# Two scaled fp16 parts for the relation matrices, the product with u as two more fold columns, and 84 instead of 90 table supertiles in a relational GNN layer

## The reference, cut to what matters

```
V = weight.reshape(in_dim, num_bases, out_dim)
W_rel = jnp.matmul(w_comp, V).reshape(num_rels, in_dim, out_dim)
h_src = h[src]
e = jnp.concatenate([h_src @ Ws.T, he @ Ws.T, h[dst] @ Ws.T], axis=1) @ Wa.T
msg = jnp.einsum('ei,eio->eo', h_src, W_rel[rel_type]) * e
h_out = jax.ops.segment_sum(msg, dst, num_segments=n_nodes)
```

## Time and profile before

| | |
|---|---|
| runs | 3934.55, 3935.9, 3939.48 us; median 3935.9 |
| profiled execution | 3944.19 us, its span 3940.3 us |
| mean granted TensorE clock | 0.951 |
| busy share of the span | PE 90%, DVE 72%, POOL 55%, ACT 34% |
| last layer with its table | about 2584 us to the end |
| matmul and table supertiles | about 2723 us to 3918 us |

### The profile page before, as it was taken

The page is one execution under the profiler, slowest core; times in us unless marked ns, Lnnn a source line. Parts: engine busy times, 40 slices in busy tenths (PEclk is TensorE's granted clock), DMA queues, the critical chain, the costliest instruction groups (busy, mean ns, idle before and its releaser), DMA issues. The chain is left out here.

```text
span 3940.3 us, 80869 instructions
## 1 busy us (share of the span) xinstructions
PE 3527.5 (90%) x29324; PEld 2108.0 (53%) x29324; DVE 2847.7 (72%) x6603; ACT 1336.1 (34%) x2952; POOL 2166.5 (55%) x3040
## 2 busy tenths in 40 slices
PE   6878878999999969999999997668999999999996
PEld 4666654544455535555555444334666666656664
DVE  8999993332221238888888786447999998888886
ACT  6899970011100013333333333044222222222221
POOL 1000001873000018888888888037888888888886
PEclk8999999999899979999999998778999999999998
DMA  6444438855255482222222222886222222222221
GB/s 163 62 91 66 87 90 331 329 201 217 86 200 201 181 284 53 60 64 60 62 62 60 57 59 68 272 292 223 53 54 53 50 54 48 50 47 48 53 48 37
DMA packets 471250, 450.98 MB, mean 114 GB/s; under 512 B 355883, under 2 KB 404171, under 8 KB 459713
## 3 DMA queue, kind: packets, MB, share of 16 engines
q1 hardware_dynamic: 392800, 397.95, 32.5%
q0 software_dynamic: 51632, 37.75, 5.9%
q10 hardware_dynamic: 26417, 10.05, 1.0%
HBM read 351.36 MB, written 95.85 MB: 113 GB/s over the span
## 5 line engine op out<-in xcount | busy, mean ns | idle before, releaser
L1815 POOL DMA_INDIRECT rows<-typed_table,ring x576 | 664.2, 1153 | 173.2 <-POOL pause L1817 153.9
L2242 PE MATMUL l_ps_g<-ring,h_part 128*128 128x512 f16 x2828 | 680.8, 381 | 36.5 <-DVE ring L2224 36.4
L1409 PE MATMUL L_ps<-ring,L_T 128*128 128x448 fp8e4 (+1 forms) x4606 | 670.5, 381 | 44.4 <-DMA ring<-adj 40.9
L1409 PEld LDWEIGHTS L_ps<-ring,L_T 128*128 128x128 f16 (+1 forms) x4606 | 327.6, 104 | 373.9 <-issue 60.2
L2248 ACT ACTIVATE l_sel<-l_ps_g 128x512 f16<-128x512 f32 x404 | 241.2, 597 | 804.4 <-PE l_ps_g L2242 793.9
L2207 POOL DMA_INDIRECT ring<-typed_table,l_idxA x384 | 420.6, 1095 | 109.2 <-POOL pause L2209 107.0
L621 PE MATMUL cells<-keys,lows 128*128 128x147 f16 (+5 forms) x2744 | 373.7, 283 | 119.3 <-DVE keys L582 104.1
L2207 POOL DMA_INDIRECT l_rows<-typed_table,l_idxA x336 | 369.3, 1099 | 99.1 <-POOL pause L2209 98.3
L2242 PEld LDWEIGHTS l_ps_g<-ring,h_part 128*128 128x128 f16 x2828 | 261.5, 98 | 295.1 <-DVE ring L2224 28.9
L1421 DVE SCALAR_TENSOR_TENSOR L_Y<-L_ps,L_scale,dinvB 128x448 f32<-128x448 f32 x84 | 57.4, 684 | 489.4 <-PE L_ps L1409 489.1
L1877 DVE TENSOR_TENSOR dinvB<-G,tyh 128x1024 f16<-128x1024 f16 x260 | 306.9, 1222 | 133.4 <-ACT G L1864 133.4
(11 more groups left out here) (371 smaller groups left out, 4810.7 us busy)
## 6 DMA issues: line engine op xcount, KB each, us to landing
ring<-adj SPq DMA_DIRECT2D x67, 2744.0 KB, 10.9
adj<-ring SPq DMA_DIRECT2D x14, 2744.0 KB, 9.2
typed_table<-ring SPq DMA_DIRECT2D x49, 765.0 KB, 7.2
ring_fifth<-src_div_mod_rows SPq DMA_DIRECT2D x130, 256.0 KB
l_krow<-src_div_mod_rows SPq DMA_DIRECT2D x101, 256.0 KB
l_trow<-type_row SPq DMA_DIRECT2D x112, 180.0 KB
attr<-in_he POOLq DMA_DIRECT2D x25, 512.0 KB, 6.3
klast<-last_keys SPq DMA_DIRECT2D x86, 128.0 KB
```

The costliest lines, as they stand in the source:

```text
L1409: ins = pe.matmul(bank[at:at + rows, 0:CH], d["T"][q][:, k, 0:rows], ring[r][:, k, :], start=n < side, stop=n >= NT - side, tile_position= ...
L1815: r_tok_[g] = r_in[b].by(pool.indirect_dma_start(rows[b][:, j, :], None, t1_dram, bass.IndirectOffsetOnAxis(ap=idxA[:, k * SUP + j:k * SUP ...
L2242: ins = pe.matmul(ps_g[p][:, 0:HE], parts[p][:, j, :], hot[b][:, j, h * HE:(h + 1) * HE], start=j == 0, stop=j == GJ - 1)
```

## The change

What it does: the relation matrices are scaled by a power of two per relation and split in two fp16 parts, written by DVE in layer 0 (`split_relations`) and no longer by POOL. The factor is taken back in the one-hot of the relation, which so becomes a compare and a multiply with a second per-partition scalar. The fold matrix gets two more columns, `u` in two fp16 parts, so that the product with `u` comes out of PE and DVE adds two columns and multiplies by a scale while it adds `termA`. `DIRECT` goes from 90 to 84.

```
-PLAIN, LEAD, DIRECT = 11, 2, 90
+PLAIN, LEAD, DIRECT = 11, 2, 84
...
+    def powers(v, top):
+
+        link(dve, dve.tensor_scalar(v[:, 0:1], v[:, 0:1], TINY, HUGE, ALU.max, ALU.min))
+        link(dve, dve.tensor_scalar(v[:, 1:2].bitcast(I32), v[:, 0:1].bitcast(I32), 0x7F800000, None, ALU.bitwise_and))
+        link(dve, dve.tensor_scalar(v[:, 2:3].bitcast(I32), v[:, 1:2].bitcast(I32), -1.0, float((254 + top) << 23), ALU.mult, ALU.add))
+        return link(dve, dve.tensor_scalar(v[:, 3:4], v[:, 1:2], 2.0 ** -top, None, ALU.mult))
...
+        def split_relations(relT, turned):
+
+            need(dve, turned)
+            link(dve, dve.tensor_reduce(rel_scale[:, 0:1], relT, AX.X, ALU.max, apply_absolute_value=True))
+            powers(rel_scale, REL_TOP)
+            link(dve, dve.tensor_scalar(rel2[:, 0, :], relT, rel_scale[:, 2:3], None, ALU.mult))
+            step(dve, dve.scalar_tensor_tensor(rel2[:, 1, :], relT, rel_scale[:, 2:3], rel2[:, 0, :], ALU.mult, ALU.subtract))
...
-            step(dve, dve.tensor_copy(fold[:, :], w("fold8")))
+            step(dve, dve.tensor_copy(fold[:, 0:F], w("fold8")))
+            link(dve, dve.tensor_reduce(u_scale[:, 0:1], t_u[:, 0:F], AX.X, ALU.max, apply_absolute_value=True))
+            powers(u_scale, REL_TOP)
+            link(dve, dve.tensor_tensor(u_each[:, 0:F], t_u[:, 0:F], w("fold8"), ALU.mult))
+            link(dve, dve.tensor_reduce(u_each[:, F:F + 1], u_each[:, 0:F], AX.X, ALU.add))
+            link(dve, dve.tensor_scalar(fold[:, F:F + 1], u_each[:, F:F + 1], u_scale[:, 2:3], None, ALU.mult))
+            step(dve, dve.scalar_tensor_tensor(fold[:, F + 1:FU], u_each[:, F:F + 1], u_scale[:, 2:3], fold[:, F:F + 1], ALU.mult, ALU.subtract))
...
-                ty_tok[i] = c_ty.by(dve.tensor_scalar(tyh[i % 3][:, :], trow[b][:, :], iotaP[0:R90, :], None, ALU.is_equal))
+                ty_tok[i] = c_ty.by(dve.tensor_scalar(tyh[i % 3][:, :], trow[b][:, :], iotaP[0:R90, :], rel_scale[:, 3:4], ALU.is_equal, ALU.mult))
...
-                        for p in range(3):
-                            ins = pe.matmul(ps_w[q][:, (j % 2) * 256:(j % 2 + 1) * 256], tyh[i % 3][:, j * P:(j + 1) * P], rel[:, p, :], start=p == 0, stop=p == 2)
+                        for p in range(2):
+                            ins = pe.matmul(ps_w[q][:, (j % 2) * 256:(j % 2 + 1) * 256], tyh[i % 3][:, j * P:(j + 1) * P], rel2[:, p, :], start=p == 0, stop=p == 1)
...
-                dve.wait_ge(*c_e.by(dve.tensor_tensor(ua[b][:, :, :], rows_of, under(t_u[:, 0:F], SUP), ALU.mult)))
-                e_tok[i] = c_e.by(dve.tensor_reduce(eP[b][:, :], ua[b][:, :, :], AX.X, ALU.add))
+                if by_matmul[i]:
+                    e_tok[i] = c_e.by(dve.tensor_tensor(eP[b][:, :], G[b][:, :, F], G[b][:, :, F + 1], ALU.add))
+                else:
+                    dve.wait_ge(*c_e.by(dve.tensor_tensor(ua[b][:, :, :], rows_of, under(t_u[:, 0:F], SUP), ALU.mult)))
+                    e_tok[i] = c_e.by(dve.tensor_reduce(eP[b][:, :], ua[b][:, :, :], AX.X, ALU.add))
```

More of the change, by code:

```diff
@@ L49 @@
 TOP = 14
+REL_TOP = 12
 TINY, HUGE = 2.0 ** -100, 2.0 ** 100
@@ L65 @@
 XW = 7 * F
+FU = F + 2
 XC = R90 * RC
 LEAD1, DIRECT1, ROWS_AHEAD = 3, 72, 12
-PLAIN, LEAD, DIRECT = 11, 2, 90
+PLAIN, LEAD, DIRECT = 11, 2, 84
 SPLIT_FROM = 4
@@ L207, in program @@
     pause = sb(life, "pause", [P, 128])
+    rel_scale = sb(life, "rel_scale", [R90, 4])
+    rel2 = rel[:, :, :].bitcast(F16)[:, 0:2, :]
     def w(name):
@@ L1588, in edge_terms @@
             make_rows(attr, s_attr[0], s_term[0])
-            split_relations(attr, s_attr[0])
-            return [(x.sem, x.n) for x in s_term]
+            return [(x.sem, x.n) for x in s_term], turn_relations(attr, s_attr[0])
         def make_rows(attr, s_part_in, s_rows):
@@ L1638, in layers_fast @@
         st = one_pass(d, 4, st, [feature(d, "fold64", 128, 64, "dec_b1"), rows_table(d, 1, "dec2", 64, F)], F)
+        split_relations(*turned_relations)
         d["spread"] = []
@@ L1679, in gather_plain_tables @@
             parts = [sb(s, f"h_part{s_load.n}_{p}", [P, GJ, KK * F], F16) for p in range(2)]
-            fold = sb(s, f"fold{s_load.n}", [P, F], F16)
-            step(dve, dve.tensor_copy(fold[:, :], w("fold8")))
+            fold = sb(s, f"fold{s_load.n}", [P, FU], F16)
+            u_each = sb(s, f"u_each{s_load.n}", [P, F + 1])
+            u_scale = sb(s, f"u_scale{s_load.n}", [P, 4])
+            step(dve, dve.tensor_copy(fold[:, 0:F], w("fold8")))
[5 more added lines that the diff above has]
+            step(dve, dve.scalar_tensor_tensor(fold[:, F + 1:FU], u_each[:, F:F + 1], u_scale[:, 2:3], fold[:, F:F + 1], ALU.mult, ALU.subtract))
             full = KK * P * (GJ - 1)
@@ L1697, in gather_plain_tables @@
                 toks.append(step(dve, dve.scalar_tensor_tensor(lo, src, HSCALE, hi, ALU.mult, ALU.subtract)))
-            return parts, fold, [toks[-1], far_tok]
+            return parts, fold, u_scale, [toks[-1], far_tok]
         def typed_layer(x_spread, HT):
@@ L2094, in relation_layer @@
             sel = [[sb(s, f"l3_sel{b}_{h}", [P, HE], F16) for h in range(2 * HALVES)] for b in range(2)]
-            G = [sb(s, f"l3_G{b}", [P, SUP, F]) for b in range(2)]
+            G = [sb(s, f"l3_G{b}", [P, SUP, FU]) for b in range(2)]
             ua = [sb(s, f"l3_ua{b}", [P, SUP, F]) for b in range(2)]
@@ L2256, in fold_rows @@
                     for p in range(2):
-                        ins = pe.matmul(ps_f[:, j * F:(j + 1) * F], sel[i % 2][2 * h + p][:, q * P:(q + 1) * P], fold[:, :], start=p == 0, stop=p == 1)
+                        ins = pe.matmul(ps_f[:, j * FU:(j + 1) * FU], sel[i % 2][2 * h + p][:, q * P:(q + 1) * P], fold[:, :], start=p == 0, stop=p == 1)
                 fold_tok[i] = c_fold.by(ins)
@@ L2264, in keep_rows @@
                     act.wait_ge(*e_tok[i - 2])
-                G_tok[i] = c_G.by(act.activation(G[i % 2][:, :, :], ps_f[:, 0:SUP * F].rearrange("p (e c) -> p e c", c=F), ACT.Copy, scale=1.0 / HSCALE))
+                G_tok[i] = c_G.by(act.activation(G[i % 2][:, :, :], ps_f[:, 0:SUP * FU].rearrange("p (e c) -> p e c", c=FU), ACT.Copy, scale=1.0 / HSCALE))
             def expand(i, half):
@@ L2281, in messages @@
                 if by_matmul[i]:
-                    rows_of, tok = G[b][:, :, :], G_tok[i]
+                    rows_of, tok = G[b][:, :, 0:F], G_tok[i]
                 else:
@@ L2305, in messages @@
                         dve.wait_ge(*e_tok[i])
-                        e = c_e.by(dve.tensor_tensor(eP[b][:, :], eP[b][:, :], termA[:, k * SUP:(k + 1) * SUP], ALU.add))
+                        if by_matmul[i]:
+                            e = c_e.by(dve.scalar_tensor_tensor(eP[b][:, :], eP[b][:, :], u_scale[:, 3:4], termA[:, k * SUP:(k + 1) * SUP], ALU.mult, ALU.add))
+                        else:
+                            e = c_e.by(dve.tensor_tensor(eP[b][:, :], eP[b][:, :], termA[:, k * SUP:(k + 1) * SUP], ALU.add))
                     else:
@@ L2350, in relation_layer @@
             x_ready = split_rows_of_h(h_tok)
-            parts, fold, part_toks = gather_plain_tables(s, stored, wide)
+            parts, fold, u_scale, part_toks = gather_plain_tables(s, stored, wide)
             make_hot(0)
```

10 lines of the change are left out of this document (3 added, 7 removed).

## The result

The changed kernel takes 3864.0 us (median of 4 runs, 3856.8 to 3874.2), the kernel before 3935.2 (4 runs, 3933.6 to 3939.5). The ratio is 0.9825, 95% interval 0.9807 to 0.9843: 1.75% faster, 71 us. The forecast was 3865. Executions more than 1.5% above the fastest of their kernel are left out of this ratio and of all later ones.

What follows compares the result with a forecast made beforehand. POOL's table fetches, held up by DVE, were taken to bound the stretch from about 2723 us, with PE and DVE almost level. POOL's sum falls from 1193.5 to 1122.7 us, so 3935.9 - 70.8 = 3865 us; range 3851 to 3893.

Steps and rivals of the forecast that it cites:

- POOL sets the end: From about 2723 us on, the end hangs on POOL's table fetches; POOL still ends last by little; chance 0.60.
- Six table supertiles fewer, 1122.7 us of fetches: POOL's fetch stream: 969.7 us undisturbed plus 107 rounds of 1.43 us delay (1.53 less 0.10), 70.8 us less than 1193.5.
- rival A: POOL is held up more, 1.72 us per round, and gains only 39.8 us: 3896 us; chance 0.17.
- The long fetch that I read: POOL fetch at 2847.14 takes 0.87 us extra, read as held by DVE's `make_dst` and product with `u`.
- PE, 1086.5 us: PE's work between first and last fold: 106 cycles of 9.36 us plus 82 times 1.15, 38 us less than before.
- Rival D: Expanding matmuls mixing bf16 one-hot and fp16 matrices run at half pace: 110 us more, 4046 us; chance 0.04.
- POOL catches DVE only at the very end: POOL, slower by 0.5 us per table supertile, uses up a lead of some 40 us; the 37 us stall nearly disappears.
- DVE stays under PE: DVE needs 10.16 and 9.17 us per cycle, with and without a table supertile, under PE's 10.51 and 9.36.
- Rival C: Second scalar takes the relation's one-hot out of fast mode, 0.76 us more, so DVE exceeds PE: 3900 us; chance 0.07.
- PE and POOL end nearly level: Last table supertile weighed at 3846.9 us behind POOL; PE and DVE would be ready at about 3834.
- B's bound: Rival: POOL fast enough at 1.24 us per round, PE ends last; at most 83.7 us less, 3852 us; chance 0.12.
- The start costs nothing: Added DVE instructions, 1.7 us before the clearing and about 2 in layer 0, are hidden; POOL starts at 2723 as before.

Runs made afterwards that it cites:

- e1: Changed kernel with the old 90 table supertiles (DIRECT 90) instead of 84; ratio to the kernel before 0.9922 (0.9898 to 0.9947).
- e2: Kernel before with 84 table supertiles instead of 90, nothing else changed; ratio to the kernel before 1.0108 (1.0058 to 1.0158).
- e9: Changed kernel, unchanged, timed again in the third call; ratio to the kernel before 0.9747 (0.9647 to 0.9846).
- e3: Changed kernel with DVE's product with u and its sum put back for matmul supertiles; ratio to the kernel before 0.9877 (0.9844 to 0.9910).
- e4: Changed kernel with 82 table supertiles instead of 84; ratio to the kernel before 0.9823 (0.9790 to 0.9855).
- e12: Changed kernel with POOL's memset after each last-layer table fetch widened from 128 to 192 columns; ratio to the kernel before 0.9798 (0.9689 to 0.9907).
- e5: Kernel before, unchanged, run again for a profile in the second call; 1282.4 us from first table fetch to the end, no ratio.
- e8: Changed kernel with 83 table supertiles instead of 84, in the second call; ratio to the kernel before 0.9739 (0.9602 to 0.9876).

## Why the prediction was right

- **POOL sets the end: right.** The last weighing is 1.2 us behind POOL before and after, e1 gains only 0.8% though each cycle of PE is lighter by as much as in the changed kernel, and e2 with fewer fetches alone is slower because PE takes over.
- **Six table supertiles fewer, 1122.7 us of fetches: right in size, 1121.2, and 1123.6 in e9.** The two things under it were not as told. I took a round at its old mean of 1.53 and gave the removal of the product 0.10. By e2 and e3 a round costs about 1.7 with the product and 84 table supertiles, nearly the 1.72 that rival A took from the first stretch, and the removal gives 0.31 back. 1.53 - 0.10 and 1.73 - 0.31 are the same 1.4. The reason for the relief was wrong too. The long fetch that I read ends at 2848.96, 0.82 us after `make_dst` and 0.62 after the product; that its extra 0.87 us is just as long as the two instructions together was chance, and only 2 fetches of e3 are held to the product's end. The box on DMAs issued by GpSimd in the Trainium skill ("SBUF — State Buffer", the two separate sides of SBUF) names only the fast instructions. The list of holders in that section also has instructions with two SBUF inputs, against GpSimd instructions that read SBUF; `make_dst` is one, and most of the held time in the two traces compared above ends with it, 75 and 88 us.
- **PE, 1086.5 us: right.** Cycles of 10.51 and 9.35 us; the folds took 10 us more. Rival D fell with the 0.109 us of an expanding matmul.
- **POOL catches DVE only at the very end: wrong.** The lead was as told, the first table row is weighed 38 us after its fetches end. But over the first 34 table supertiles POOL took 13.6 us each and DVE used one every 12.5, so the lead was gone at 3186 us, less than half way. From about 3250 us DVE waits some 2.2 us for a row once in 53 us. This costs little: PE's first idle time over 0.3 us comes at 3465 us.
- **DVE stays under PE: right, by less than I said.** The second scalar costs 0.06 us and the scaling at `termA` another 0.06, so DVE needs some 10.3 us and not 10.16. Rival C, 0.76 us, is out.
- **PE and POOL end nearly level: right.** With 82 instead of 84 the stretch is 4.7 us longer, in another call (e4). B's bound, 83.7 us less, was not reached.
- **The start costs nothing: not measurable.** From the copy to the clearing are 1.87 us, where it was 0.12, and ACT issued the load 1.7 us after the clearing, so it still waited for something else. In layer 0 the next instruction of the chain comes 1.6 us later than it did, against a bound of 1.3. The same program starts the plain fetches of the last layer at 2579.0 us here and at 2591.6 in e9, so a cost of this size cannot be seen in the time.

The two places on which these readings of the start rest:

```profile
2574.51 0.17 DVE L1698 CAST fold<-W 128x16 f16<-128x16 f32 x1
...
2576.38 0.19 DVE L1708 MEMSET h_part<- 128x64 uint32 x2
...
2578.26 0.40 ACTq L1713 DMA_DIRECT2D ring<-h_rows  x1
```

```profile
1339.99 0.34 DVE L1353 SCALAR_TENSOR_TENSOR L_T<-L_tmp,L_scale,L_T 128x112 f16<-128x112 f32 x1 [0.53 <-ACT L_T L1352]
...
1342.68 0.68 DVE L1432 SCALAR_TENSOR_TENSOR L_Y<-L_ps,L_scale,dinvB 128x448 f32<-128x448 f32 x1 [0.39 <-PE L_ps L1420]
```

That the figure came within 1 us is luck in part: two errors of about 20 us each cancelled, and single executions of the changed kernel spread over 17 us.

## What to carry to other kernels

Where two engines share work that can go either way, sum up each one's stream from its own first to its own last instruction, not by busy shares: PE was busy 100% for nearly half the stretch, yet the end hung on a POOL that was 82% busy. A saving on one of them is worth something only with the split moved, and the two steps have to be judged together (0.992 and 1.011 alone, 0.9825 together). What one engine's instructions cost another per round is measured by putting one such instruction back: a single long fetch showed a third of it and the wrong cause. Then compare where the delayed instructions end in both traces, since an instruction that changes the rhythm can cost more than one that holds.

## What had not been expected of the hardware

- A DVE product of 128 elements on two SBUF tensors, 0.27 us long, lengthens POOL's indirect fetches by 0.31 us per round on the mean (e3), yet only 2 of them, 1.6 us, end with it. Nine tenths of the held time end 0.82 to 0.85 us after `make_dst` or the first addition of a weighing, in kernels with and without the product, and what they lose depends on the moment at which they meet these: a memset wider by 0.05 us alone brought 26 us of longer fetches (e12).
- The same kernel took 3935, 3976, 4076 and 4088 us in four calls. By the record the chip was the same, number 15, in the calls with 3976 and 4076, so the chip alone does not tell them apart. In the two profiles of the kernel before (3944.2 and 4051.3 us) two places account for the difference: from the first plain fetch to the first table fetch, while 37 MB of table are stored, 129 us in the first and 170 in e5 (129 in the changed kernel's first profile too, 154 to 164 in the other runs); and the stretch, 65 us longer in e5. There PE has 62 us of idle time that nothing in the profile explains, and its granted clock is 0.98 instead of 1.00. What slows PE there stays open.
- The memset of a scratch tile between fetches looks like waste, and in that call was not: with 16 columns in place of 128 POOL's steps fell from 1.44 to 1.35 us, and the kernel became 3% slower than the one before, 5.5% slower than e8, which keeps the 128 columns. Why is not shown.
